# Transposed attention scores summed up over differences of keys, with 64-row second passes side by side

## The reference

```python
x = x + attn(layernorm(x), Wq, Wk, Wv, Wo, bo)
x = x + ffn(layernorm(x), w_gate, w_up, w_down)
# attn, for each batch and head, N = 1024, d = 64
sim = q @ k.T * d ** -0.5
e = exp(sim - max(sim, axis=-1))
out = (e / (sum(e) + 1e-10)) @ v          # then @ Wo.T + bo
# ffn, every product with both operands quantised to FP4 in blocks of 16
h = silu(fp4_linear(x, w_gate)) * fp4_linear(x, w_up)
y = fp4_linear(h, w_down)
```

## Time and profile before

| | |
|---|---|
| median of 3 runs | 1536.1 us (1535.93 to 1537.97) |
| profiled execution, its own time | 1537.8 us |
| its span, first to last instruction | 1535.9 us |
| mean granted TensorE clock | 0.985 of full speed |
| busy: PE, DVE, ACT, POOL | 1465.5, 1090.2, 1162.8, 1247.4 us |

### The profile page before, as it was taken

How to read it: one execution, slowest core, us unless ns; L and a number is a source line. 1 busy time by engine, 2 the same in 40 slices (tenths; PEclk the granted TensorE clock), 3 DMA queues, 4 the chain that set the end, 5 groups by cost and what they waited for, 6 DMA issues and landing times.

```text
span 1535.9 us, 35256 instructions
## 1 busy us (share of the span) xinstructions
PE 1465.5 (95%) x13828; PEld 971.5 (63%) x13828; DVE 1090.2 (71%) x1717; ACT 1162.8 (76%) x2413; POOL 1247.4 (81%) x1391
## 2 busy tenths in 40 slices
PE   4999999999999999999999999999999999999965
PEld 2566666666666666666666666666666666666644
DVE  7666676677667777686776767677676767767567
ACT  3788888877777777777777778777777877777832
POOL 4888989888888888787888878788888888878942
PEclk8999999999999999999999999999999999999987
DMA  6111110101111111111110111111111111111000
GB/s 166 43 42 43 43 42 22 42 23 43 43 42 43 32 35 27 43 43 46 43 26 23 46 43 42 46 28 37 25 46 43 43 43 25 26 42 46 1 4 14
DMA packets 46660, 59.77 MB, mean 39 GB/s; under 512 B 8672, under 2 KB 21920, under 8 KB 46496
## 3 DMA queue, kind: packets, MB, share of 16 engines
q1 hardware_dynamic: 46336, 57.26, 15.9%
q10 hardware_dynamic: 160, 0.26, 0.1%
HBM read 4.80 MB, written 2.10 MB: 4 GB/s over the span
## 4 chain that ended last, share of the span: by engine, by line
PE 81%; DVE 11%; ACT 4%; issue 2%; POOL 1%; DMA 1%; SPq 0%; DVEq 0%
PE ob L633 26%; PE st L605 15%; PE st L607 12%; PE sm L586 10%; PE mb L522 5%; PE mb L538 4%; DVE negm L939 3%; PE mb L527 2%; PE mb L1239 2%; PE mb L533 1%; ACT probs L759 1%; POOL p_low L449 1%; PE mb L1250 1%; PE mb L551 1%; DVE qv L1110 1%
## 5 line engine op out<-in xcount | busy, mean ns | idle before, releaser
L449 POOL TENSOR_TENSOR p_low<-probs 128x512 f16<-128x512 f32 x1024 | 1086.2, 1073 | 226.1 <-ACT probs L759 219.2
L759 ACT ACTIVATE probs<-st,lift,exp_scale 128x512 f32<-128x512 f32 x1024 | 793.4, 775 | 199.9 <-PE st L607 181.1
L939 DVE TENSOR_REDUCE negm<-sm 128x1 f32<-128x1024 f32 x508 | 617.9, 1216 | 162.6 <-PE sm L586 161.2
L605 PE MATMUL st<-q_hl,k_hh 128*128 128x512 f16 x1024 | 393.8, 385 | 2.3 <-DMA q_hm<-m_low 2.3
L607 PE MATMUL st<-q_hm,k_l 128*128 128x512 f16 x1024 | 388.5, 379 | 0.0
L633 PEld LDWEIGHTS ob<-v,p_low 128*128 128x128 f16 x4096 | 275.2, 97 | 123.0 <-POOL p_low L449 3.3
L633 PEld LDWEIGHTS ob<-v,probs 128*128 128x128 bf16 x4096 | 276.1, 98 | 120.7 <-ACT probs L759 0.5
L633 PE MATMUL ob<-v,p_low 128*128 128x129 f16 x4096 | 316.6, 219 | 2.5 <-POOL p_low L449 2.4
L633 PE MATMUL ob<-v,probs 128*128 128x129 f16 x4096 | 317.5, 220 | 0.2
L586 PE MATMUL sm<-k_hh,q_hl 64*128 64x512 f16 x508 | 197.1, 388 | 17.7 <-DVE negm L939 17.7
L586 PE MATMUL sm<-k_hh,q_hm 64*128 64x512 f16 x508 | 197.3, 388 | 0.0
(11 more groups left out here) (175 smaller groups left out, 1539.4 us busy)
## 6 DMA issues: line engine op xcount, KB each, us to landing
k_hh<-k_high SPq DMA_DIRECT2D x128, 128.0 KB, 2.3
k_l<-k_low SPq DMA_DIRECT2D x64, 128.0 KB, 2.3
q_hl<-q_high SPq DMA_DIRECT2D x64, 128.0 KB, 2.3
q_hl<-q_low SPq DMA_DIRECT2D x64, 128.0 KB, 2.4
q_hm<-q_high SPq DMA_DIRECT2D x62, 128.0 KB, 2.3
x<-x SPq DMA_DIRECT2D x4, 512.0 KB, 7.2
q_hm<-m_high SPq DMA_DIRECT2D x128, 1.0 KB
q_hm<-m_low SPq DMA_DIRECT2D x128, 1.0 KB
```

Source lines behind the costliest of these rows:

```text
L449: return pool.tensor_tensor(p_low[b][:, j, :], p, p.bitcast(BF16)[:, 1::2], ALU.subtract)
L605: pe.matmul(st[s % 2][:, :], k_hh[n][:, s * P:(s + 1) * P], q_hl[n][:, half * HALF:(half + 1) * HALF], start=True, stop=False)
L759: nc.scalar.activation(probs[k % 2][:, s, :], st[s % 2][:, :], ACT.Exp, bias=lift[:, 0:1], scale=exp_scale[:, head, pair:pair + 1]).then_i ...
L939: nc.vector.tensor_reduce(negm[k % 2][:, s // 2:s // 2 + 1], banks[:, :, :].rearrange("p a n -> p (a n)"), AX.X, ALU.max, negate=True).the ...
```

## The change

S^T of key tile s is no longer computed afresh. Slots 0 and 1 are as before. From slot 2 on, the bank still holds S^T of tile s - 2 with its maximum, and the passes add the product of q with the difference of the keys of tile s and tile s - 2. For that k is projected, from tile 2 on, from xTd, the transposed difference of normalised x between tiles two apart (POOL makes it in xnd, new jobs E0, E1 for batch 0 and e0, e1 in rounds 3, 5, 7 transpose it and split it in high and low). k0's matmuls are each cut in two of 256 columns.

The second pass of slots from 2 on needs no maximum and so only 64 rows: low_pair does that of an even slot and of the odd slot after it side by side, from row halves of k_l and of q_hl and q_hm, into both st banks at once, and it stands in the even slot behind the score pair, which moves from the odd to the even slots. It waits for the exponent of the slot before.

The maxima still need the keys themselves: new jobs y0, y1 project the high parts only (one pass a half, taken by ScalarE alone into y_parts, four transfers into k_y) at the places where k0 and k1 stood. k0 and k1 go to slots (2,3) and (2,5), v0 and v1 to (2,7) and (3,5), on other banks than before. k's transfers become ten (four high, six low) and stand behind the store in SyncE's queue.

On VectorE the reduction is in even slots, ahead of the slot's jobs; on ScalarE the sums and the scaling of outputs stand ahead of the exponent of slots 0, 4 and 2, 6.

```diff
-JOBS = [("k0", 0, (0, 1), (0, 2), (0, 2)), ("m", 1, (0, 1), (0, 2), (0, 2)), ("k1", 1, (0, 3), (0, 4), (0, 4)),
+JOBS = [("y0", 0, (0, 1), (0, 2), None), ("m", 1, (0, 1), (0, 2), (0, 2)), ("y1", 1, (0, 3), (0, 4), None),
         ("q0", 0, (0, 5), (0, 6), (0, 6)), ("t0", 0, (0, 7), (1, 0), None), ("m", 0, (1, 1), (1, 2), (1, 2)),
-        ("q1", 1, (1, 1), (1, 2), (1, 2)), ("o0", 0, (1, 3), None, (1, 4)), ("x", 0, (1, 5), (1, 6), None),
-        ("t1", 1, (1, 5), (1, 6), None), ("g0", 0, (1, 7), (2, 0), (2, 2)), ("h0", 0, (1, 7), (2, 0), None),
-        ("w2", 0, (1, 7), (2, 0), None), ("o1", 1, (1, 7), None, (2, 0)), ("m", 1, (2, 1), (2, 2), (2, 2)),
-        ("u0", 1, (2, 3), None, (2, 4)), ("h1", 1, (2, 3), (2, 4), None), ("w0", 1, (2, 3), (2, 4), None),
-        ("v0", 0, (2, 3), (2, 4), (2, 4)), ("g1", 0, (2, 7), (3, 0), (3, 2)), ("d", 0, (2, 7), None, (3, 0)),
-        ("n0", 0, (2, 7), (3, 0), (3, 0)), ("w1", 0, (2, 7), (3, 0), None), ("v1", 1, (2, 7), (3, 0), (3, 0)),
-        ("u1", 1, (3, 1), None, (3, 2)), ("m", 1, (3, 3), (3, 4), (3, 4)), ("n1", 0, (3, 3), (3, 4), (3, 4))]
+        ("q1", 1, (1, 1), (1, 2), (1, 2)), ("E0", 1, (1, 3), (1, 4), (1, 4)), ("o0", 0, (1, 3), None, (1, 4)),
+        ("E1", 0, (1, 5), (1, 6), (1, 6)), ("x", 0, (1, 5), (1, 6), None), ("t1", 1, (1, 5), (1, 6), None),
+        ("g0", 0, (1, 7), (2, 0), (2, 2)), ("h0", 0, (1, 7), (2, 0), None), ("w2", 0, (1, 7), (2, 0), None),
+        ("o1", 1, (1, 7), None, (2, 0)), ("m", 1, (2, 1), (2, 2), (2, 2)), ("u0", 1, (2, 3), None, (2, 4)),
+        ("h1", 1, (2, 3), (2, 4), None), ("w0", 1, (2, 3), (2, 4), None), ("k0", 0, (2, 3), (2, 4), (2, 4)),
+        ("k1", 1, (2, 5), (2, 6), (2, 6)), ("g1", 0, (2, 7), (3, 0), (3, 2)), ("d", 0, (2, 7), None, (3, 0)),
+        ("n0", 0, (2, 7), (3, 0), (3, 0)), ("e0", 0, (2, 7), (3, 0), (3, 0)), ("v0", 1, (2, 7), (3, 0), (3, 0)),
+        ("u1", 1, (3, 1), None, (3, 2)), ("w1", 0, (3, 1), (3, 2), None), ("m", 1, (3, 3), (3, 4), (3, 4)),
+        ("n1", 0, (3, 3), (3, 4), (3, 4)), ("e1", 0, (3, 3), (3, 4), (3, 4)), ("v1", 0, (3, 5), (3, 6), (3, 6))]
...
             if name[0] == "n":
-                return s_xe, 2 * (g // 2) + c + 1
+                return s_xe, 4 * (g // 2) + c + 1
+            if name[0] in "eE":
+                return s_xe, 4 * (g // 2) + 2 + c + 1
...
-                    wait(sp, s_hi, 4 * g + 2)
+                    wait(sp, s_y, 2 * g + 2)
                     for h in range(2):
-                        high = k_parts[0][h * DH:(h + 1) * DH, :]
-                        sp.dma_start(k_hh[n + h][0:DH, :], high).then_inc(s_dkh[h], 16)
-                        sp.dma_start(k_hh[n + h][DH:P, :], high).then_inc(s_dkh[h], 16)
-
-                    wait(sp, s_lo, 4 * g + 2)
-                    for h in range(2):
-                        sp.dma_start(k_l1[n + h][DH:P, :], k_parts[1][h * DH:(h + 1) * DH, :]).then_inc(s_dkl[h], 16)
+                        for c in range(2):
+                            sp.dma_start(k_y[n + h][c * DH:(c + 1) * DH, :],
+                                         y_parts[h * DH:(h + 1) * DH, c * HALF:(c + 1) * HALF]).then_inc(s_dy[h], 16)
                 if cur:
                     place_max(1)
                 if nxt:
 
-                    wait(sp, s_hi, 4 * g + 4)
+                    wait(sp, s_hi, 4 * g + 2)
                     for h in range(2):
                         high = q_parts[0][h * DH:(h + 1) * DH, :]
                         sp.dma_start(q_hl[n + h][0:DH, :], high).then_inc(s_dqh[h], 16)
                         if r:
                             sp.dma_start(q_hm[n + h][DH:P, :], high).then_inc(s_dqh[h], 16)
 
-                    wait(sp, s_lo, 4 * g + 4)
+                    wait(sp, s_lo, 4 * g + 2)
                     for h in range(2):
                         sp.dma_start(q_hl[n + h][DH:P, :], q_parts[1][h * DH:(h + 1) * DH, :]).then_inc(s_dql[h], 16)
                 if cur:
@@ -366,6 +381,21 @@
                 if ffn_two(r, 2) is not None:
                     ffn.store(sp, out_t, s_out, x2, ffn_two(r, 2))
                 if nxt:
+
+                    wait(sp, s_hi, 4 * g + 4)
+                    for h in range(2):
+                        high = k_parts[0][h * DH:(h + 1) * DH, :]
+                        sp.dma_start(k_hh[n + h][0:DH, :], high).then_inc(s_dkh[h], 16)
+                        sp.dma_start(k_hh[n + h][DH:P, :], high).then_inc(s_dkh[h], 16)
+
+                    wait(sp, s_lo, 4 * g + 4)
+                    for h in range(2):
+                        low = k_parts[1][h * DH:(h + 1) * DH, :]
+                        sp.dma_start(k_l[n + h][DH:P, 0:2 * P], low[:, 0:2 * P]).then_inc(s_dkl[h], 16)
+                        pairs = low[:, 2 * P:N].rearrange("d (t two j) -> d two t j", two=2, j=P)
+                        for two in range(2):
+                            sp.dma_start(k_l[n + h][two * DH:(two + 1) * DH, 2 * P:].rearrange("d (t j) -> d t j", j=P),
+                                         pairs[:, two, :, :]).then_inc(s_dkl[h], 16)
                     place_max(3)
...
+            def differences(b):
+
+                pool.wait_ge(s_xn, 4 * (b + 1))
+                wait(pool, s_xe, 4 * b)
+                pool.tensor_tensor(xnd[:, :, :], xn[:, 2:TB, :], xn[:, 0:TB - 2, :], ALU.subtract).then_inc(s_xd, 1)
...
+            def turn_differences(bank, b, c):
+
+                pe.wait_ge(s_xd, b + 1)
+                for t in range(2 + 2 * c):
+                    last = pe.transpose(bank[:, t * P:(t + 1) * P], xnd[:, 2 * c + t, :], ident[:, :])
...
+                if name[0] == "y":
+                    last = pe.matmul(bank[:, :], of_pair(wT[0], 1, g), of_batch(xT[0], g, c * HALF, HALF), start=True, stop=True)
+                elif name[0] == "q":
 
                     for w, a in ((0, 0), (0, 1), (1, 0)):
-                        last = pe.matmul(bank[:, :], of_pair(wT[w], "qk".index(name[0]), g), of_batch(xT[a], g, c * HALF, HALF),
+                        last = pe.matmul(bank[:, :], of_pair(wT[w], 0, g), of_batch(xT[a], g, c * HALF, HALF),
+                                         start=(w == 0 and a == 0), stop=(w == 1))
+                elif name == "k0":
+
+                    for w, a in ((0, 0), (0, 1), (1, 0)):
+                        pe.matmul(bank[:, 0:2 * P], of_pair(wT[w], 1, g), of_batch(xT[a], g, 0, 2 * P),
+                                  start=(w == 0 and a == 0), stop=False, skip_group_check=True)
+                        last = pe.matmul(bank[:, 2 * P:4 * P], of_pair(wT[w], 1, g), of_batch(xTd[a], g, 0, 2 * P),
+                                         start=False, stop=(w == 1), skip_group_check=True)
+                elif name == "k1":
...
-                        if k % 2 == 0 and s == 1:
-                            wait(pe, s_dkh[h], 32 * (g + (1 if k else 0)))
+                        if k % 2 == 0 and s == 0:
+                            wait(pe, s_dy[h], 32 * (g + (1 if k else 0)))
                             wait(pe, s_dqh[h], 32 * (g + (1 if k else 0)))
                         pair = 4 * (unit + 2) + s // 2
                         if r == 0:
@@ -583,30 +648,56 @@
                         t = half * IT + s // 2
                         for h, q_rows in enumerate((q_hl[n], q_hm[n])):
                             rows = slice(h * DH, (h + 1) * DH)
-                            last = pe.matmul(banks[:, h, :], q_rows[rows, t * P:(t + 1) * P],
-                                             k_hh[n][rows, h * 512:(h + 1) * 512], start=True, stop=True)
+                            last = pe.matmul(banks[:, h, :], q_rows[rows, t * P:(t + 1) * P], k_y[n][rows, :],
+                                             start=True, stop=True)
                         last.then_inc(s_sm, 2)
+
+                    def first_pass(n, s, begin):
+
+                        wait(pe, s_ex, 32 * (g - 1) + 8 * k + s - 1)
+                        return pe.matmul(st[s % 2][:, :], k_hh[n][:, s * P:(s + 1) * P],
+                                         q_hl[n][:, half * HALF:(half + 1) * HALF], start=begin, stop=False,
+                                         skip_group_check=True)
+
+                    def low_and_max(n, s):
+
+                        return pe.matmul(st[s][:, :], k_l[n][:, s * P:(s + 1) * P],
+                                         q_hm[n][:, half * HALF:(half + 1) * HALF], start=False, stop=True,
+                                         skip_group_check=True)
+
+                    def low_pair(n, s):
+
+                        wait(pe, s_ex, 32 * (g - 1) + 8 * k + s)
+                        cols = slice(P + s // 2 * P, 2 * P + s // 2 * P)
+                        for two, q_rows in enumerate((q_hl[n], q_hm[n])):
+                            rows = slice(two * DH, (two + 1) * DH)
+                            last = pe.matmul(st[two][:, :], k_l[n][rows, cols], q_rows[rows, half * HALF:(half + 1) * HALF],
```

(53 more changed lines are left out.)

79 lines of the change are left out of this document (57 added, 22 removed).

## The result

The changed kernel takes **1658.5 us** (median of four runs, 1657.2 to 1659.5) against 1537.0 for the kernel before in four runs beside it (1535.9 to 1538.3): ratio **1.079, interval 1.0771 to 1.0808**. The forecast was slower, 1598, range 1550 to 1625. The direction came out; of 121.5 us it had 62. The profiled execution took 1659.5 us, its span 1657.7.

A forecast was written before the change was run, and what follows sets the result against it. TensorE's order was taken as the bound: its saved stream would be lost to bank waits and SyncE's queue. Terms 1 + 31 + 22 + 5 + 3 = +62 on 1536.1 gave 1598 us, range 1550 to 1625.

The forecast's parts named there:

- Second passes and TensorE's stream: TensorE: 64-row pairs save 85 us, y adds 14, so its stream falls by 71 us, 2.27 a full round.
- k0's halves: TensorE: splitting k0 into 256-column matmuls changes no column count; taken as 0, at most 0.3 us a round.
- The bank waits: TensorE waits for banks VectorE frees only after the reduction: 0.60 behind q_low, 0.18 behind m_low, 0.66 behind k_low.
- Even rounds: Even FFN rounds 10 to 32: bank waits of 5.0 us minus 2.27 saved, +2.7 a round, 31 us in all.
- SyncE's queue: End of odd FFN rounds: store waits for d's addition, ten k transfers and the maximum follow; next round starts at 47.7.
- Odd FFN rounds: Rounds 11 to 31: SyncE's queue decides, 47.7 us against 45.65 before, +2.05 each, 22 us in all.
- the start-up: k0's and k1's lows delay VectorE's maxima and ten k transfers stand ahead in SyncE's queue: +3 us (0 to 5).
- Rounds 1 to 9: Rounds before steady feed-forward work: +1 us from bank waits, +5 from LayerNorm rounds 2 to 7, together +6.
- Rival 1: The gain arrives: banks come free in time on VectorE, giving 1468 us, or about 1505 with half the waits; chance 0.10.
- Rival 2: Only the banks cost time, not SyncE's queue in odd rounds: without the 22 us, 1576 us; chance 0.13.
- Rival 3: Evacuation becomes the bound: low pairs wait for exponents or miss the score pair's switch, 1615 to 1640 us; chance 0.10.
- the exponents' loop: Low pairs write both banks, so wait for the previous slot's exponent on ScalarE; taken as 0, upper bound 75 us.

The follow-up runs named there:

- experiment 1: Changed kernel with VectorE taking the projection banks before the row maximum in each slot instead of after it: 1594.8 us, ratio 1.0382.
- experiment 4: Kernel before with only the score pairs and reductions moved to even slots, no low pairs or differences: 1585.4 us, ratio 1.0315.
- experiment 8: Changed kernel without the low pairs (second passes of slots 2 to 7) and their wait for the exponent: 1655.8 us, ratio 1.0767.
- experiment 2: Changed kernel with the store of finished tiles behind the row maximum in SyncE's queue: 1642.3 us, ratio 1.0687.
- experiment 5: Changed kernel with the quantiser's lift steps on ScalarE one slot later, in even slots: 1655.0 us, ratio 1.0765.
- experiment 10: Changed kernel with store last, lifts later, slot-5 reciprocals in slot 4, soonest-wanted banks taken before the reduction, t0 on the other bank, q0 behind: 1527.5 us, ratio 0.9939.

## Why the prediction came out as it did

*Second passes and TensorE's stream (-71).* Right in kind, somewhat too large. Low pairs start 0.21 to 0.23 behind score pairs, and a slot pair with its job's first matmul next is 1.99 long (711.74 to 713.73), forecast 1.975. A round saves 1.8, not 2.27: about 57 us in all. 12 x 0.015 explains 0.2 of the difference. The other 0.3 lies in jobs that take 0.04 to 0.05 longer than before, six in an even round: t0, x, o0, u0, g1 and u1 (t0 takes 0.49 instead of 0.44), all but g1 right behind a wait. k0's halves cost nothing: 0.65 for six, as for three whole passes before.

*The bank waits.* Right, mechanism and size: 0.60 was 0.63, wait by wait, and experiments 1, 4 and 8 (its even rounds) confirm it by removing, isolating and stretching it. Even rounds came out at +3.4 for +2.7, of which 0.5 is the stream's term and 0.2 this one. The rounds from 1 to 6 without a quantiser came out at +0.8 to +2.2 for +0.1 to +1.2, rounds 2, 4 and 6 at +0.8 for +0.6. In round 3 (+2.0 for +1.2) the six transpositions of differences take 0.65, as forecast (0.6); beside the stream's term o1's wait of 0.29 was missing, and a part of v0's 0.47 behind e0. Round 1 (+2.2 for +0.1) is mostly the clock: granted 0.92 of full speed on its average, 1.00 before.

*SyncE's queue.* The tail from d's addition was exact (9.2 for 9.3), and the store's place is worth 16 us by experiment 2. This forecast summed the whole odd round through that one tail, so all that was missed ahead of the addition came on top of it.

*Odd FFN rounds (+2.05): this is the step that failed*, a term mis-sized by 3.3 in most of them, 40 us of the 60 that are missing (the rest: 14 in rounds 1 to 9, 8 in even rounds, 1 in the start-up, less 4 at the end). "Only the two lift steps [...] hold it: inside the odd rounds, where SyncE's queue covers it. I take 0." That is true of the lift at (3,3), as experiment 5 shows, and false of that at (0,5): it stands ahead of d's addition, so the tail starts later by the 1.60 it costs. y1 adds another 1.5 to its 1.0, since the quantiser has a piece ahead of the reduction of slot 0 as well as one behind it. Together they are 3.1 of the 3.4 by which the addition came late. That the wait has two causes in series was in no term: remove the lifts alone and t0's bank takes back 1.0 of the 1.60.

*Rounds 1 to 9 (+6).* The same omission: rounds 5 and 8 quantise weights in slots (1,0) to (1,6), and I put nothing there. In round 8 o0 waits 2.64 for m_low, which stands behind five quantiser operations, one of them 2.07 long, and the weight's transposition waits 2.5. The two rounds make 10 of the 20 us; some 1.6 of round 8 is the clock behind the first wait (last section). Round 9 (+2.0) already holds x's quantiser: a low pair waits 1.53 for its exponent.

*Rivals.* Rival 1, the gain arrives, is out; experiment 10 shows that in another order the kernel with the pairs is 0.6% faster than the kernel before. No run gave the kernel before the same lift steps, store and reciprocals, so how much of these 10 us is the passes' is open. Rival 2 is out: the queue was in it, for 16 us. Rival 3's sign, TensorE's waits naming exponents, did appear (36.7 us), and its figure of 1615 to 1640 was nearest to the result, though the range ended at 1625; but the exponents' loop was not the cause, for without these waits (experiment 5) the kernel takes 1655.0 and without any low pair (experiment 8) 1655.8. The waits came by the lift steps, which are program order again. The Trainium skill, TensorEngine Tiling (Array Packing), PSUM Bottleneck, which spoke against this change, is borne out in this form: 64-row pairs freed TensorE of 1.8 us a round, and the kernel was slower until the order of the engines that empty the banks, and of SyncE's queue, was changed (1658.5 in the one order, 1527.5 in the other).

## What to carry to other kernels

When a change moves a long instruction ahead of short ones that free a buffer, price the buffer's release against the moment at which the other engine wants it, at every place, and sum these; that was right here within 0.07 at each place where one taking follows one reduction; where two do, count both. Do the same for everything else behind the moved instruction, the quantiser pieces, small reciprocals and the other engine's steps that wait for them, also where a later queue seems to cover them: cover counts only for what lies behind the point at which the covering queue starts. And before the idea is dropped, try the two or three orders of the releasing engine: the same passes ran at 1.079 and at 0.994 of the kernel before.
